# A two-layer attention and FFN kernel on one core: tile work of one sequence placed between the attention steps of the other, records made per key group

## The chip, the cores and the metric

One core of a Trainium2 chip. The time is device microseconds (us) of one execution, the median of the runs shown; less is better. Engines: PE is TensorE, DVE is VectorE, ACT is ScalarE, POOL is GpSimd, SP is SyncE, which issues the transfers. Each runs its own instructions in order, and they wait for each other through semaphores.

## The reference

Input x is 2 sequences of 1024 tokens with 512 features, fp32. Four residual blocks follow each other; attention has 32 query heads of 16 and 8 key/value heads (4 query heads to a key/value head), is causal, and rotates q and k by position. The FFN has one matrix of ±1 and a scale.

```
x = x + attn_a(layernorm(x), w_qkv_a, w_o_a)
x = x + scale * (layernorm(x) @ (2 * kernel - 1))
x = x + attn_b(layernorm(x), w_qkv_b, w_o_b)
x = x + scale * (layernorm(x) @ (2 * kernel - 1))
```

## The kernel before

**Four rounds.** A round is one sequence through one layer; the order is sequence 0 layers a and b, then sequence 1 layers a and b. The whole sequence lives in `xs` (8 tiles of 128 tokens). A round has three stages.

**Stage A** (`SLOTS_A`, one slot per tile): layer norm statistics (`ln_stats` L976, `ln_newton` L990), the transpose of the normed tile, its split into a high part (`hi` L834, ACT) and a low part (`lo` L1009, DVE), the projection to 768 q, k, v columns in three products (`qkv` L572, `multiply` L558), the rotation (`rope_sin` L1204 on POOL, `rope_cos` L1035 and `rope` L1046 on DVE). Then `part_h` L872 (ACT) and `part_l` L1217 (POOL) write a **record** of 64 numbers for each head: the value in parts whose products give fp32 precision. PE transposes a tile's records of all heads in six quads (`turn_rec` L594), and ACT and DVE copy them to `qT` and `kT`, which hold all 8 key groups. Units of group 0 (below) are already made in this stage.

**Groups** 0 to 7, one for each key/value head with its 4 query heads. A **unit** (`unit` L617 on PE, L1052 on DVE) computes scores of a query tile, and DVE reduces them to row maxima (L1068); 22 units make a group. The maxima are split on POOL, transposed on PE (`nm_turn`), copied, and brought by a transfer (`put_nm` L477) as extra rows into `qT`. The **score steps** S.0 to S.17 (`scores` L662) compute scores transposed with the maximum already subtracted; ACT applies Exp to two heads or pairs at a time (L905); POOL cuts diagonal blocks (`mask` L1259); PE multiplies with the values (`pv` L680, ten steps). The output is transposed back (`o_turn`), and divided on DVE (`o_divide`). While group g is in its score steps, the units of g+1 run. The order is written by hand: `GROUP_ORDER` L175, `FIRST_ORDER` L185 for group 0, `LAST_ORDER` L195 for group 7, where no units are left and the first tiles of the next stage stand in their place.

**Tail** (`TAIL_ORDER` L205): per tile the output projection (C: transpose CT, 12 matmuls CP, add), layer norm, FFN (D: transpose DT, 8 matmuls DP, add), with the start of the next round's stage A.

**PSUM.** Of eight banks `psM` has four: in groups they are two pairs, and units, N and O jobs take them by turns (`ring_jobs` L268); a job's pair is free when DVE has read it. In stage A the early units have one of the pairs only (`unit_pair` L256), and the projections the other. `psE` has three banks for score steps, `psO` one for the outputs.

Weights are loaded each round: qkv in one transfer into the `probs` buffer (L467) and split in the tail, the output matrix in four pieces in groups 1 to 4.

Of the kernel before, what the change touches and what calls it, by code (L numbers as in the profile page):

```python
# [37 lines left out]

# [8 lines left out]
RECS = 2  # L47
QUADS = 6
QUAD_ACT = [1, 2, 4, 5]
QUAD_DVE = [0, 3]  # L50

AHEAD = TILES // 2
# [4 lines left out]

CD_TILES = words("C.0 C.1 C.2 C.3 D.0 D.1 C.4 C.5 C.6 C.7 D.2 D.3 D.4 D.5 D.6 D.7")
TURNS = TILES + len(CD_TILES)


def c_turn(t):
    return TILES + CD_TILES.index(("C", t))


def d_turn(t):
    return TILES + CD_TILES.index(("D", t))


assert all(X % 2 == t % 2 for X, (what, t) in enumerate(CD_TILES)) and CD_TILES[-1] == ("D", TILES - 1)


class Signal:

    def __init__(self, sem, credit=0):
        self.sem, self.credit = sem, credit

    def after(self, n):

        return n + (self.credit + 1)  # L90
# [49 lines left out]

# [50 lines left out]
LAST_ORDER = """  # L195
S.0 PV.8.-1 S.1 PV.9.-1 N.1.0 S.2 OC.1.-1 S.3 S.4 PV.0.0
S.5 PV.1.0 S.6 O.1.-1 OC.0.0 PV.2.0 S.7 O.0.0
S.8 CT.0 S.9 PV.3.0 CT.1 S.10 CP.0 PV.4.0
S.11 CT.2 S.12 CP.1 LS.0 S.13 PV.5.0 CT.3 LN.0
S.14 CP.2 S.15 PV.6.0 DT.0 LR.0 S.16 CP.3 S.17 PV.7.0 DT.1 LS.1 LM.0 PV.8.0 PV.9.0  # L200
"""

TAIL_ORDER = """  # L205
DP.0 LN.1 LR.1 O.1.0 DP.1 LM.1 CT.4 CT.5 CP.4 CT.6 CP.5 CT.7 LS.2 T.2 CP.6 T.3 H.2 LN.2 LR.2 LM.2
# [7 lines left out]

# [1135 lines left out]
```

## Time and profile before

| | |
|---|---|
| median of 3 runs | 1418.94 us (1417.74 to 1422.94) |
| profiled execution, span from first to last instruction | 1417.0 us |
| PE busy, weight loads (PEld) | 1296.8 us (92%), 773.8 us (55%) |
| DVE busy | 1039.4 us (73%) |
| ACT busy | 941.6 us (66%) |
| POOL busy | 382.3 us (27%) |
| mean granted clock of PE | 0.988 |

A row of a window view gives, for a stretch of the span, the busy time of each engine in it. A row of the timeline gives a start, a duration from the start of the first to the end of the last instruction of the row, and the instructions merged into it. Matmuls are pipelined and their ends are modelled, so what a matmul costs the engine that is never idle is the distance from its start to the start of the next, not its duration.

### The profile page before, as it was taken

To read this page: it belongs to the slowest core of one execution; us is meant where nothing else is said; L and a number is where in the kernel's file an instruction comes from. 1 tells how busy PE (TensorE), PEld (TensorE's weight loads), DVE (VectorE), ACT (ScalarE), POOL (GpSimd) and SP (SyncE) were. 2 spreads that over 40 slices of the span, in tenths; PEclk is the share of its full clock that TensorE was granted. 3 is DMA by queue.
4 is the path that set the end of the run, shared out by engine and by line. 5 is a ranking of instruction groups with operands and counts; after the bars stand their busy time and mean duration, and the time that the engine had idled before them with its cause. 6 is when DMAs were issued, how large, how long until landed. Compare 5 with 4: busy or idle time off the path is not lost.

```text
span 1417.0 us, 28602 instructions
## 1 busy us (share of the span) xinstructions
PE 1296.8 (92%) x11076; PEld 773.8 (55%) x11076; DVE 1039.4 (73%) x1526; ACT 941.6 (66%) x1770; POOL 382.3 (27%) x591
## 2 busy tenths in 40 slices
PE   5988999989898899998989789999998889999898
PEld 4764444446785444444677444444477744444456
DVE  5667888845767788883566879889266588888737
ACT  4655777774665687776556567877646566877764
POOL 3431222210443122221144222222123422222212
PEclk9999999999999999999999999999999999999999
DMA  3000000001000000000220000000010000000002
GB/s 124 1 1 10 9 18 3 3 2 45 1 1 2 9 13 15 3 2 2 75 90 1 2 10 17 11 2 3 2 45 1 1 2 17 10 10 3 3 6 100
DMA packets 12981, 24.00 MB, mean 17 GB/s; under 512 B 1072, under 2 KB 4144, under 8 KB 12848
## 3 DMA queue, kind: packets, MB, share of 16 engines
q1 hardware_dynamic: 12848, 22.19, 4.7%
q8 instruction: 88, 1.44, 0.4%
q14 instruction: 45, 0.37, 0.1%
HBM read 16.94 MB, written 4.19 MB: 15 GB/s over the span
## 4 chain that ended last, share of the span: by engine, by line
PE 59%; DVE 25%; ACT 7%; issue 5%; POOL 2%; DMA 1%; DVEq 0%; ACTq 0%; SPq 0%; POOLq 0%
DVE mx L1068 18%; PE psO L696 15%; PE psM L560 12%; PE psE L675 12%; PE psM L633 10%; PE psM L543 3%; ACT probs L905 3%; PE psE L613 3%; PE psO L613 2%; PE psM L640 2%; DVE stats L983 2%; POOL attn L1213 1%; DVE qT L1033 1%; DVE xs L1144 1%; ACT xn L823 1%
## 5 line engine op out<-in xcount | busy, mean ns | idle before, releaser
L1068 DVE TENSOR_REDUCE mx<-psM 128x2 f32<-128x768 f32 (+4 forms) x704 | 698.2, 1026 | 113.9 <-PE psM L640 68.4
L905 ACT ACTIVATE probs<-psE 128x512 f32<-128x512 f32 x1152 | 625.5, 595 | 228.5 <-PE psE L675 219.0
L633 PE MATMUL psM<-kT,qT 62*128 62x384 f32 (+5 forms) x1536 | 294.8, 404 | 31.3 <-DVE mx L1068 9.5
L696 PE MATMUL psO<-probs,v_grp 128*32 128x512 f32 (+3 forms) x3072 | 318.5, 503 | 2.3 <-POOL probs L1266 2.2
L1266 POOL TENSOR_SCALAR_AFFINE_SELECT probs<-probs 128x512 f32<-128x512 f32 x256 | 159.3, 634 | 561.7 <-ACT probs L905 527.4
L675 PE MATMUL psE<-qT,kT 64*128 64x512 f32 (+3 forms) x1536 | 279.7, 401 | 32.5 <-ACT probs L905 26.7
L633 PEld LDWEIGHTS psM<-kT,qT 62*128 62x128 f32 x1536 | 146.4, 187 | 179.3 <-DVE mx L1068 133.9
L675 PEld LDWEIGHTS psE<-qT,kT 64*128 64x128 f32 x1536 | 131.3, 186 | 171.2 <-ACT probs L905 126.2
L640 PE MATMUL psM<-mask_b 64*128 64x64 bf16 x2048 | 120.7, 197 | 0.0
L560 PE MATMUL psM<-wq_hi,xT_hi 128*128 128x512 f32 (+1 forms) x384 | 99.1, 380 | 14.7 <-ACT vs L869 9.5
L696 PEld LDWEIGHTS psO<-probs,v_grp 128*32 128x32 f32 x3072 | 68.1, 109 | 65.3 <-issue 36.9
L560 PE MATMUL psM<-w_lo,xT_hi 128*128 128x512 f32 (+1 forms) x384 | 93.6, 366 | 2.0 <-DVE w_lo L1022 2.0
L560 PE MATMUL psM<-wq_hi,xT_lo 128*128 128x512 f32 (+1 forms) x384 | 93.1, 365 | 0.0
L640 PEld LDWEIGHTS psM<-mask_b 64*128 64x128 bf16 x2048 | 60.4, 97 | 56.9 <-issue 25.2
L1213 POOL TENSOR_TENSOR attn<-attn,sin_s 128x320 f32<-128x320 f32 x64 | 66.6, 1061 | 50.8 <-ACT attn L868 50.8
L560 PEld LDWEIGHTS psM<-wq_hi,xT_hi 128*128 128x128 f32 x384 | 62.3, 192 | 28.5 <-issue 18.9
L839 ACT ACTIVATE xT_hi<-psM 128x512 fp32r<-128x512 f32 x64 | 37.8, 597 | 58.5 <-PE psM L543 38.8
L1222 POOL TENSOR_TENSOR probs<-attn,probs 128x512 fp32r<-128x512 f32 x32 | 41.2, 1289 | 125.5 <-ACT probs L880 125.5
L1013 DVE TENSOR_TENSOR xT_lo<-psM,xT_hi 128x512 fp32r<-128x512 f32 x64 | 43.6, 686 | 39.7 <-ACT xT_hi L839 39.1
L613 PE MATMUL psE<-ident,probs 128*128 128x128 f32 x384 | 60.4, 281 | 12.9 <-DVE qT L1033 11.1
L560 PEld LDWEIGHTS psM<-w_lo,xT_hi 128*128 128x128 f32 x384 | 64.8, 191 | 12.9 <-DVE w_lo L1022 2.7
L560 PEld LDWEIGHTS psM<-wq_hi,xT_lo 128*128 128x128 f32 x384 | 65.0, 192 | 9.9
(81 smaller groups left out, 1240.6 us busy)
## 6 DMA issues: line engine op xcount, KB each, us to landing
probs<-in_w_qkv SPq DMA_DIRECT2D x5, 1536.0 KB, 6.4
xs<-in_x SPq DMA_DIRECT2D x8, 512.0 KB, 3.9
xn<-in_w_o SPq DMA_DIRECT2D x16, 256.0 KB, 2.6
out_x<-xs SPq DMA_DIRECT2D x8, 512.0 KB, 2.8
qT<-nm_rows SPq DMA_DIRECT2D x128, 8.0 KB
probs<-in_w_ffn SPq DMA_DIRECT2D x1, 256.0 KB, 7.3
attn<-in_mask SPq DMA_DIRECT2D x1, 160.0 KB, 9.4
sin_s<-in_sin SPq DMA_DIRECT2D x1, 128.0 KB, 6.8
```

What stands on the lines that cost most here:

```text
L543: ins = pe.transpose(dst[:, c * P:(c + 1) * P], src[:, c * P:(c + 1) * P], ident[:])
L560: ins = pe.matmul(dst, xT[:, k, c, :], w[:, c, n0:n1], start=first and i == 0, stop=last and i == len(some) - 1)
L613: ins = pe.transpose(bank[:, n * P:(n + 1) * P], src, ident[:])
L633: return pe.matmul(psM[:, 2 * pair + h % 2, to:to + k1 - k0], qT[lo:lo + MAXROW, g, qt // QT_PER_CHUNK, h // 2, qt % QT_PER_CHUNK * P:(qt ...
L640: return pe.matmul(psM[:, 2 * pair + h % 2, k0:k0 + P // 2], late_b[lo:lo + ROW, half, :], half_b[lo:lo + ROW, :], start=False, stop=half ...
L675: ins = pe.matmul(psE[:, (2 * p + a) % SRING, to:to + w], kT[lo:lo + DEPTH, g, kb * P:(kb + 1) * P], qT[lo:lo + DEPTH, g, c, j // 2, off:o ...
L696: ins = pe.matmul(psO[VW * j:VW * (j + 1), off:off + w], v_grp[:, kb, :], probs[:, (g * NS + s) % PSLOTS, at(j), to:to + w], start=s in (0 ...
L905: act.activation(probs[:, (g * NS + s) % PSLOTS, at(heads[0]):at(heads[0]) + len(heads), 0:w], psE[:, n % SRING, 0:w * len(heads)].rearran ...
L1013: dve.tensor_tensor(xT_lo[:, k].rearrange("p a b -> p (a b)"), src, xT_hi[:, k].rearrange("p a b -> p (a b)").bitcast(F32), ALU.subtract). ...
L1068: dve.tensor_reduce(to, src, AX.X, ALU.max, negate=True).then_inc(ring_used.sem, 1)
L1213: ins = pool.tensor_tensor(t4[:, :, a, :], x4[:, :, 1 - a, :], sn[:, :, a * HALF:(a + 1) * HALF].to_broadcast([P, HEADS + KV, HALF]), ALU. ...
L1266: ins = pool.affine_select(out=d, in_=d, compare_op=ALU.is_ge, fill=0.0, base=0, pattern=[[0, REP], [1, P]], channel_multiplier=-1)
```

## The change

**Rounds.** The order of rounds is now layer a of sequence 0, layer a of sequence 1, layer b of sequence 0, layer b of sequence 1. While round k is in its groups, the other sequence goes, two tiles (a **pair**) at a time, through output projection, FFN and norm of its last attention (where it has one) and the qkv projection of its next (where it has one). So round 0 carries qkv work alone, rounds 1 and 2 all of it, round 3 output and FFN alone. Before the first group stands a prologue (sequence 0's qkv, then records and units of group 0), and behind the last the output work of sequence 1.

**One program for all engines.** A list of words (`PROGRAM`) is made from tables, and each engine walks it and issues its part. `PAIR_ORDER` puts a pair's words behind score steps, counted from the pair's first; pairs begin 26 steps apart, and a round has 144 steps. CT, DT and AT are the transposes of a pair (8 of 128x128), each followed at once by H, its high and low copy (1024 wide); CP has 6 pieces of four matmuls, DP 4, Q 4 for each tile; CA and DA add to x, QC copies q, k, v out; LS, LN, LM are the norm; RO is the rotation.

**PSUM.** `ring_pairs` deals the two pairs of `psM` to all jobs: units, N, O, R, transposes and projections. A projection holds its pair from its first piece to CA, DA or QC, and until then every other job has the other pair alone. In the table of rounds 1 and 2 a pair is held at 56 of 144 steps, and 65 of 176 units, 10 N, 6 O and 7 R jobs fall there; in round 0 it is 24 steps with 27 units, 4 N, 2 O and 5 R; in round 3 (its first seven groups) 32 steps with 38 units, 6 N, 4 O and 2 R.

**Records** are made per group two groups ahead: `PL` (high parts on ACT L853, low on POOL L1110) over all tiles, and three jobs R of 8 transposes each, two copied by ACT and one by DVE, 1024 wide. `qT` and `kT` hold three groups instead of eight. The rotation works in place in `cells`, so its cosine part now waits for POOL's sine part.

**Transfers.** `xs` holds three pairs; x goes through DRAM (`x_mid`) between layers: 24 loads and 16 stores of 512 KB in place of 8 and 8. Weights have buffers of their own and are loaded once for each layer in pieces, 12 after the start in place of 20 transfers.

The core of the diff (the tables and what deals out PSUM):

```diff
-GROUP_ORDER = """
-U.0 U.1 S.0 N.1.0 PV.8.-1 S.1 U.2 PV.9.-1 OC.1.-1 S.2 U.3 U.4 S.3 U.5 S.4 PV.0.0 S.5 U.6 U.7 PV.1.0
-S.6 U.8 O.1.-1 S.7 U.9 PV.2.0 OC.0.0 U.10 S.8 U.11 PV.3.0 U.12 S.9 O.0.0 S.10 U.13 N.0.1 S.11 U.14
-U.15 S.12 PV.4.0 U.16 S.13 U.17 PV.5.0 U.18 S.14 U.19 PV.6.0 S.15 U.20 U.21 S.16 PV.7.0 S.17 X
-"""
+GROUP_ORDER = """
+U.0 S.0 N.1.0 PV.8.-1 U.1 S.1 U.2 PV.9.-1 V OC.1.-1 S.2 U.3 S.3 U.4 U.5 S.4 PV.0.0 S.5 U.6 PV.1.0 U.7
+S.6 U.8 O.1.-1 S.7 U.9 PV.2.0 OC.0.0 U.10 S.8 K.0 U.11 PV.3.0 U.12 S.9 O.0.0 S.10 U.13 N.0.1 PL S.11 U.14
+U.15 S.12 PV.4.0 U.16 S.13 U.17 PV.5.0 U.18 S.14 R.0 U.19 PV.6.0 S.15 R.1 U.20 U.21 S.16 R.2 PV.7.0 S.17 X K.1
+"""
+START, PERIOD = 7, 26
+PAIR_ORDER = """
+0 LX CT H.CT | 2 CP.0 | 3 CP.1 | 4 CP.2 | 5 CP.3 | 6 CP.4 | 7 CP.5 CA LS.D | 9 LN.D LM.D | 10 DT H.DT | 12 DP.0 | 13 DP.1 | 14 DP.2
+| 15 DP.3 DA ST LS.A | 17 LN.A LM.A | 18 AT H.AT | 19 Q.0.0 | 20 Q.0.1 | 21 Q.0.2 | 22 Q.0.3 QC.0 | 23 Q.1.0 RO.0 | 24 Q.1.1 | 25 Q.1.2
+| 26 Q.1.3 QC.1 | 28 RO.1
+"""
...
+def ring_pairs():
+
+    pair_of, before, held, newest, turn = {}, {}, {}, [None, None], 1
+    for w in PROGRAM:
+        what = w[0]
+        job = None
+        if what in ("U", "N", "O", "R", "CT", "DT", "AT"):
+            job = w
+        elif what in ("CP", "DP") and w[2] == 0:
+            job = w[:2]
+        elif what == "Q" and w[3] == 0:
+            job = w[:3]
+        if job is not None:
+            turn = 1 - turn if 1 - turn not in held.values() else turn
+            assert turn not in held.values(), w
+            pair_of[job], before[job], newest[turn] = turn, newest[turn], job
+            if what not in ("U", "N", "O", "R"):
+                held[job] = turn
...
-        xs = sb("xs", [P, TILES, DIM])
+        xs = sb("xs", [P, XSLOTS, 2, DIM])
...
-        qT = sb("qT", [P, KV, CHUNKS, REP // 2, QCHUNK], F32R)
-        kT = sb("kT", [P, KV, SEQ], F32R)
+        qT = sb("qT", [P, 3, CHUNKS, REP // 2, QCHUNK], F32R)
+        kT = sb("kT", [P, 3, SEQ], F32R)
...
+            def part_h(G):
+                r, g = G // KV, G % KV
+                src = by_group(cells, r, g)
+                act.wait_ge(rope_ready, ROPE_NO[r * PAIRS + PAIRS - 1, 1] + 1)
```

**PE in a group in mid round.** L675 and L749 are score steps, L633 and L708 with L640 and L715 the units and their masks, L696 and L769 the value products, L660 the transposed maxima. Before:

```order
L675 MATMUL psE<-qT,kT 128x384 x2
L675 MATMUL psE<-qT,kT 128x128 x2
L696 MATMUL psO<-probs,v_grp 32x512 x4
L633 MATMUL psM<-kT,qT 128x448 x2
L675 MATMUL psE<-qT,kT 128x512 x2
L633 MATMUL psM<-kT,qT 128x448 x2
L640 MATMUL psM<-mask_b 128x64 x4
```

Now, in round 1 (L622 is a piece of a projection, L780 the transposed output):

```order
L749 MATMUL psE<-qT,kT 128x512 x2
L622 MATMUL psM<-wq_hi,xT_hi 128x512 x4
L708 MATMUL psM<-kT,qT 128x320 x2
L780 MATMUL psM<-ident,o_T 128x128 x4
L749 MATMUL psE<-qT,kT 128x512 x2
L622 MATMUL psM<-wq_lo,xT_hi 128x512 x4
L708 MATMUL psM<-kT,qT 128x320 x2
L715 MATMUL psM<-mask_b 128x64 x4
L769 MATMUL psO<-probs,v_grp 32x256 x4
L708 MATMUL psM<-kT,qT 128x384 x2
L749 MATMUL psE<-qT,kT 128x512 x2
L622 MATMUL psM<-wq_hi,xT_lo 128x512 x4
```

A piece of four matmuls stands behind each score step, and its bank pair is not given back before the last piece has been copied out.

**DVE in the same part of a group.** L1068 and L1026 are the reductions of units. Before:

```order
L1068 TENSOR_REDUCE mx<-psM 128x2
L1081 CAST nm_rows<-psM 32x128
L1068 TENSOR_REDUCE mx<-psM 128x2 x8
L1074 TENSOR_TENSOR mx<-mx 128x16
L1068 TENSOR_REDUCE mx<-psM 128x2x2 x2
```

Now, in round 1 (L1001 and L1003 are the rotation, L974 a low copy, L1008 the copy of the key records):

```order
L1026 TENSOR_REDUCE mx<-psM 128x2 x2
L1001 TENSOR_TENSOR cells<-cells,cos_s 128x8x80
L1003 TENSOR_TENSOR cells<-cells,t_s 128x8x80
L1026 TENSOR_REDUCE mx<-psM 128x2 x4
L974 TENSOR_TENSOR xT_lo<-psM,xT_hi 128x1024
L1026 TENSOR_REDUCE mx<-psM 128x2 x2
L1008 CAST kT<-psM 128x1024
L1001 TENSOR_TENSOR cells<-cells,cos_s 128x8x80
L1003 TENSOR_TENSOR cells<-cells,t_s 128x8x80
L1032 TENSOR_TENSOR mx<-mx 128x16
```

The reductions, which stood in one row of eight, now have rotation, low copy and record copy between them.

## Rows read from the trace of the kernel before

**Rows 1.** The page: span, and busy time of each engine.
```profile
span 1417.0 us, 28602 instructions
PE 1296.8 (92%) x11076; PEld 773.8 (55%) x11076; DVE 1039.4 (73%) x1526; ACT 941.6 (66%) x1770; POOL 382.3 (27%) x591
```

**Rows 2.** Windows: prologue; groups 0 and 4; group 7 to next group 0; the end.
```profile
core 0: us, PE busy (x) PEld busy (x) DVE busy (x) ACT busy (x) POOL busy (x), PEclk, DMA share, GB/s
0.00:101.60 101.60, 78.99 (x521) 65.05 (x523) 61.12 (x103) 54.36 (x101) 38.86 (x44) 0.97 0.13 44
101.60:135.60 34.00, 27.75 (x285) 14.06 (x283) 28.74 (x34) 20.14 (x37) 6.21 (x14) 0.96 0.04 10
...
217.40:244.00 26.60, 25.83 (x267) 12.60 (x267) 23.58 (x30) 20.93 (x39) 7.35 (x14) 1.00 0.02 4
...
297.20:449.70 152.50, 138.29 (x916) 102.89 (x909) 88.65 (x171) 88.97 (x171) 46.81 (x50) 1.00 0.03 12
1341.10:1417.00 75.90, 67.30 (x399) 44.07 (x391) 37.52 (x90) 41.56 (x80) 12.54 (x13) 1.00 0.14 50
```

**Rows 3.** Timeline of PE in group 4: start, us, engine, line, operation.
```profile
218.17 0.49 PE L675 MATMUL psE<-qT,kT 64*128 64x512 f32 x2
218.50 0.35 PE L633 MATMUL psM<-kT,qT 62*128 62x384 f32 x2
...
218.86 1.06 PE L696 MATMUL psO<-probs,v_grp 128*32 128x512 f32 x8
219.86 0.50 PE L675 MATMUL psE<-qT,kT 64*128 64x384 f32 x4
220.20 0.39 PE L633 MATMUL psM<-kT,qT 62*128 62x384 f32 x2
...
220.50 0.47 PE L633 MATMUL psM<-kT,qT 62*128 62x512 f32 x2
```

**Rows 4.** Waits in group 4: who for whom, us, times, longest.
```profile
PEld psM L633 <- DVE mx L1068: 4.3, 9, 0.8
```

**Rows 5.** Timeline of DVE in group 4.
```profile
218.97 0.96 DVE L1068 TENSOR_REDUCE mx<-psM 128x2 f32<-128x768 f32 x1 [0.30 <-PE psM L640]
```

**Rows 6.** Chain of waits in the first 102 us: pieces of projections.
```profile
51.68 0.93 PE psM L560 x4
...
55.28 1.43 PE psM L560 x12
```

**Rows 7.** Timeline of PE in stage A: transposes of records.
```profile
54.24 0.60 PE L613 MATMUL psE<-ident,probs 128*128 128x128 f32 x4
54.68 0.60 PE L613 MATMUL psO<-ident,probs 128*128 128x128 f32 x4
```

**Rows 8.** Groups by line and shape: mean ns behind the busy us.
```profile
L1068 DVE TENSOR_REDUCE mx<-psM 128x2 f32<-128x1024 f32 x192 | 225.4, 1217 | 4.6 <-PE psM L633 4.2
...
L1213 POOL TENSOR_TENSOR attn<-attn,sin_s 128x320 f32<-128x320 f32 x64 | 66.6, 1061 | 50.8 <-ACT attn L868 50.8
...
L1013 DVE TENSOR_TENSOR xT_lo<-psM,xT_hi 128x512 fp32r<-128x512 f32 x64 | 43.6, 686 | 39.7 <-ACT xT_hi L839 39.1
...
L1042 DVE TENSOR_TENSOR attn<-attn,cos_s 128x640 f32<-128x640 f32 x32 | 27.7, 867 | 57.8 <-ACT attn L868 56.9 <-DVE var_eps L988 0.9
...
L1144 DVE SCALAR_TENSOR_TENSOR xs<-psM,rstd,xs 128x512 f32<-128x512 f32 x32 | 23.9, 747 | 3.0 <-DVE var_eps L988 2.3 <-DVE rstd L1000 0.7
```

**Rows 9.** Timeline of DVE: a norm's statistics, and the last steps of its Newton iteration.
```profile
340.68 0.15 DVE L994 TENSOR_TENSOR newton<-rs 128x2 f32<-128x2 f32 x1
...
341.60 0.22 DVE L1000 SCALAR_TENSOR_TENSOR rstd<-rs,scale_s,newton 128x2 f32<-128x2 f32 x1
...
349.51 1.27 DVE L983 BATCH_NORM_STATS2 stats<-xs 128x6 f32<-128x512 f32 x2
...
351.33 0.17 DVE L988 TENSOR_SCALAR var_eps<-mv 128x2 f32<-128x2 f32 x1
```

**Rows 10.** DMA issues: count, size and us to landing.
```profile
xs<-in_x SPq DMA_DIRECT2D x8, 512.0 KB, 3.9
```

More of the change, by code:

```diff
@@ L46 @@
 DEPTH = ROW
[L47 to L55, printed above, removed]
+ROUNDS = BATCH * LAYERS
+GROUPS = ROUNDS * KV
+SSTEPS = 18
+FIRST_PAIR, LAST_PAIR = -1, ROUNDS
+XSLOTS = 3
+CELL = (REP + 2) * HD
+QKCELL = (REP + 1) * HD
+GW = REP * HD
+RJOBS_ACT = 2
 def words(text):
     return [(w.split(".")[0], *(int(a) for a in w.split(".")[1:])) for w in text.split()]
[L64 to L90, printed above, removed]
 def score_steps():
@@ new lines, in pair_word @@
+def pair_word(q, name):
+    what, *arg = name.split(".")
+    arg = [int(a) if a.isdigit() else a for a in arg]
+    if what == "H":
+        return [(what, (arg[0], q))]
+    if what in ("LS", "LN", "LM"):
+        return [(what, (arg[0], q))]
+    if what in ("CT", "DT", "AT"):
+        return [(what, q)]
+    if what == "CP" and not arg:
+        return [(what, q, i) for i in range(6)]
+    if what == "DP" and not arg:
+        return [(what, q, i) for i in range(4)]
+    if what == "Q" and len(arg) == 1:
+        return [(what, q, arg[0], i) for i in range(4)]
+    return [(what, q, *arg)]
@@ new lines, in prepare_words, with program @@
+def prepare_words(text):
+    out = []
+    for what, *arg in words(text):
+        out.append((what, *arg) if what in ("PL", "V", "R") else (what, 0, *arg))
+    return out
+def program():
+    out = edge_words(PROLOGUE, FIRST_PAIR) + prepare_words(PREPARE)
+    middle = middle_words()
+    for G in range(GROUPS - 1):
+        out += group_words(G, GROUP_ORDER, middle)
+    assert not middle, sorted(middle)
+    return out + edge_words(LAST_ORDER, LAST_PAIR) + edge_words(TAIL_ORDER, LAST_PAIR)
@@ L552, in products @@
-            def products(k, his, los, n0, n1):
-                return [(xT_hi, w, c, n0, n1) for w in (his, los) if w is not None for c in range(KC)] + [
-                    (xT_lo, his, c, n0, n1) for c in range(KC)]
-            def multiply(k, dst, some, first, last):
-                for i, (xT, w, c, n0, n1) in enumerate(some):
-                    ins = pe.matmul(dst, xT[:, k, c, :], w[:, c, n0:n1], start=first and i == 0,
-                                    stop=last and i == len(some) - 1)
-                return ins
@@ L955, in _, with norm @@
-            ln_apply(0, 0)
-            first_rstd(0, 0)
-            hi(0, 0, psE[:, 0, :])
-            for c in range(KC):
-                wq_split(0, c)
-            rounds(act, round_)
+            def norm(e, q):
+                what, i = e, NORM_NO[e, q]
+                job = earlier_turn((what + "T", q), ("DT", "AT"))
+                if job is not None:
+                    act.wait_ge(turned, TURN_NO[job] + 1)
+                act.wait_ge(var_ready, i + 1)
+                for n in range(2):
+                    ins = act.activation(xn[buffer_of(q)][:, n, :], xs[:, q % XSLOTS, n, :], ACT.Identity, bias=mv[:, i % 2, n, 0:1], scale=-1.0)
+                ins.then_inc(xn_ready, 1)
```

1483 lines of the change are left out of this document (701 added, 782 removed).

## The prediction

> **What bounds the kernel now.** First the engines' sums: PE is busy 92% of the span, DVE 73%, ACT 66% [rows 1]. Then the windows, to see that the stages have different limits [rows 2]. A group in the middle takes 26.60 us with PE busy 25.83 and DVE 23.58. The stretch from the start of group 7 to the start of the next round's group 0 takes 152.5 us with PE busy 138.3, but DVE only 88.7 and ACT 89.0. The matter is what PE needs, since its busy time is modelled, so I went to the timeline. A score step costs 0.33 us from start to next start (218.17 to 218.50), or 0.34 with two parts; a unit with its mask 0.30 (220.20 to 220.50), a longer one up to 0.4; a value product of 512 columns 1.00 [rows 3]. For a group: 18 score steps x 0.34 = 6.1; 22 units x 0.37 = 8.1; ten value products, eight at 1.0 and two of half the columns at 0.57 (estimate) = 9.1; two N and two O jobs about 1.0. Sum 24.3 us, 91% of 26.60. So in a group PE (24.3) and DVE (23.6) are both near full, and PE stands still for short waits on DVE: 4.3 us of weight loads waiting for a reduction, mostly under running matmuls [rows 4].
>
> In the stretch between: four matmuls of 512 columns cost 0.93 us, twelve of 256 columns 1.43 [rows 6], four transposes 0.44 [rows 7]. The qkv projection of a tile is 3 x 0.93 + 1.43 = 4.22, of eight 33.8; output projection 24 x 0.93 = 22.3; FFN 16 x 0.93 = 14.9; 24 transposes of tiles x 0.44 = 10.6; 48 of records x 0.44 = 21.1; group 7 without units 16.2; the units of group 0 8.1. Sum 127 us of 152.5, that is 83%. The rest is PE waiting in chains of copies. This is what the change can win, together with the slow group 0 (34.00 us) [rows 2], four times each.
>
> The Trainium skill (Perfetto Trace Analysis, Identifying the Most-Contended Engine) says that matmul busy time doesn't tell how near TensorE is to its limit, and that the busy share of weight loads does. The trace agrees with the first half: 25.83 us busy against 24.3 needed. By the second, with weight loads at 55%, the time would go by DVE; that is a rival below.
>
> **The change, part by part.** Work is neither added nor removed on PE except for batching: transposes go in eights, 2 x 0.44 = 0.88.
>
> *PE.* Groups: 8 x 24.3 = 194.4 per round. Records, 24 jobs x 0.88 = 21.1. Round 0 also carries qkv, 33.8, and four pair transposes, 3.5: 252.8. Rounds 1 and 2 carry everything, 71.0, and twelve pair transposes, 10.6: 297.1 each. Round 3 has seven groups here, 170.1, 18 record jobs 15.8, output and FFN 37.2, eight pair transposes 7.0: 230.1. Together 1077.1 us between the first score step and the last group.
>
> *DVE.* A group stays at 23.58 [rows 2]. The copy of key records, 1024 wide, I price as a reduction of 1024 from PSUM, 1.22 [rows 8]. A norm takes 2.0 for statistics (349.51 to 351.50) and 1.14 for Newton (340.68 to 341.82) [rows 9]; a low copy of 1024, 1.22; adding the output projection 1.22; the FFN's 2 x 0.75; the rotation, two passes like the 0.87 one, 1.73 for each tile [rows 8]. A pair thus adds 3.1 + 1.2 + 3.5 = 7.8 in round 0, 6.3 + 3.7 + 1.2 + 1.5 + 3.5 = 16.2 in rounds 1 and 2, 3.1 + 2.4 + 1.2 + 1.5 = 8.2 in round 3. Rounds: 8 x 24.8 + 31 = 229; 263; 263; 7 x 24.8 + 33 = 207. DVE is below PE in each. Where it was 97% of PE's need in a group, it is 89% in rounds 1 and 2. Two new waits sit in its queue with all reductions behind them: for ACT's high copy at each pair's turn (48 times; now 39.1 us for 64 and shorter ones [rows 8]), and for POOL's sine, two of 1.06 us [rows 8], once a tile.
>
> *ACT and POOL* have room: ACT 20.93 of 26.60, POOL 7.35 [rows 2]. ACT gains per group about 4 us of record parts and record copies, and 4 us of copies and norms, for a group that gets 10 us longer. POOL gets the sine, 2.1 us a tile, ahead of masks; the value product of a step comes two or three score steps after its mask is asked for, over 4 us, which covers it. Without this cover PE would wait up to 2 us a tile, 24 times.
>
> *SP.* 24 more transfers of x, each landing in about 4 us [rows 10]; a load is asked for six score steps before it is used, over 8 us, so I cost it at nothing. The stores stand before later transfers of maxima, but their data are ready when SP comes to them.
>
> *The bank pairs.* Held steps: 56 + 56 + 24 + 32 = 168 of 558. A unit then waits for the reduction of the unit before. From its start to DVE's start is 0.47 us (218.50 to 218.97) [rows 3, 5], the reduction about 1.03 (23.6 with little else, for 22), 0.1 back: 1.6. In round 1: 65 x 1.6 + 10 N x 0.75 + 6 O x 1.4 + 7 R x 2.1 = 135 us of chain, against PE's need at these 56 steps, 56 x 1.35 + 6.2 + 70.8 = 153. PE has enough else to do (a score step and a piece are 1.3 us, the reduction 1.0), so the chain is mostly covered, but not where two units stand together or only a value product is between them. This eats what DVE's lighter load gives.
>
> So how full will PE be? Ends: 83% as in the stretch between (chains everywhere), and 94% (the shortest waits only). I take 90%, just under the group's 91%, since that row has the same in-order mix: 1077.1 / 0.90 = 1197.
>
> *The ends.* Prologue: 18 us to the first full projection, as now; eight tiles at 4.22 + 0.44 and small stalls, 40; rotation, parts and records of group 0 in a chain, 13; its 22 units alone, bound by DVE, 23.6 / 0.9 and a record copy, 28: 99, against 101.6. Last group and output work are as before, by pairs instead of tiles: 78 against 75.9. Together 177. The wins there are nothing.
>
> Sum: 1197 + 177 = 1374 us of span, against the profiled 1417.0. The median is 1.9 above that span, so **1376**.
>
> **The rivals.**
>
> 1. *PE fuller.* The pieces fill every wait of attention, and PE stands at 94%: 1146 + 177 = 1323. For it: DVE's share falls from 97% to 89% of PE's. Against: the two new waits and held pairs. 0.17.
> 2. *DVE is the limit, not PE* (the skill's rule above, read from the weight loads). DVE's rounds are 962 us; at the 89% of a group, 1081 + 177 = 1258. Against: a value product of 512 columns costs 1.00 us whatever waits. 0.08.
> 3. *The gain goes into chains.* In-order coupling stays at 87%, between group and stretch: 1238 + 177 = 1415, no change that can be told (about 0.5%, 7 us, is what a measurement of this kernel can tell). 0.10.
> 4. *Slower: one pair of banks binds.* Where a pair is held, pieces don't run under reductions but ahead of them. The forecast has 153 / 0.9 = 170 us for 56 held steps, 3.0 a step. With DVE's rotations and adds in the chain, 135 + 23, and half of the 71 us of pieces outside it, it is 194, or 3.46 a step. That is 0.43 x 168 = 72 more: 1446. It turns slower than before from 3.3 a step. Before, every job in a group could rotate through two pairs; nothing in the trace shows a group's units on one. 0.15.
>
> The Trainium skill (Perfetto Trace Analysis, Matmuls) asks that independent groups of matmuls rotate through different PSUM banks, so that the evacuation of one runs under the matmuls of the next. That speaks for rival 4, which breaks this at 30% of the steps.
>
> **How the numbers follow.** The forecast, PE between 88% and 92%, has 0.50. Faster: 0.50 + 0.17 + 0.08 = 0.75; no change 0.10; slower 0.15. The low end leaves out rival 2 and the best of rival 1, the high end the worse half of rival 4: 1308 to 1436. The forecast's own range is 1348 to 1401.
>
> **What would show it.** Right: the round from first score step to first score step is about 281 us for round 0, 330 for 1 and 2; PE's waits in them are short and on DVE; the time to the first score step is near 99. Held steps near 3.0 us, others near 1.8. Wrong: rounds 1 and 2 over 345 with weight loads of units waiting for reductions (rival 4), or below 315 (rivals 1 and 2, the second with DVE at 89% busy); PE waiting for masks or for maxima brought by transfers, which I cost at nothing.

## The result, and the profile after

| | before | after |
|---|---|---|
| median of 4 runs | 1420.72 us | 1850.41 us (1848.78 to 1857.28) |
| ratio, 95% interval | | 1.304 (1.3015 to 1.3066) |
| profiled span | 1417.0 us | 1849.7 us |
| mean granted clock of PE | 0.988 | 0.903 |

The change makes the kernel 30% slower; 1376 was forecast. From the page of the changed kernel, the counterpart of [rows 1]: the sums, and the row of PE's granted clock in 40 slices, in tenths.

```profile
span 1849.7 us, 28067 instructions
...
PE 1474.2 (80%) x11072; PEld 817.5 (44%) x11072; DVE 1041.2 (56%) x1415; ACT 905.8 (49%) x1601; POOL 334.3 (18%) x565
...
PEclk9769898998998989888999898988889988999999
```

No engine got more work: PE has 11072 matmuls where it had 11076, DVE is busy for 1041 us where it was 1039. Yet PE's busy time is 177 us longer, and PE's idle time is 375 us where it was 120, 255 more. These two make up the 433 us between the spans. Most of the 177 us is the clock: in the trace 311.5 us of PE's busy time lie in stretches at the lower level, before 32.5, and half of the difference, about 140 us (an estimate), is by how much those matmuls would be shorter at full clock.

The windows after: time to the first score step; the four rounds, each from its first score step to the next one's (the fourth without its last group); then three single groups, and the end. Columns as in [rows 2].

```profile
0.00:113.40 113.40, 75.78 (x399) 59.00 (x399) 58.01 (x90) 29.54 (x44) 23.86 (x33) 0.78 0.11 39
113.40:485.30 371.90, 303.06 (x2525) 162.16 (x2525) 228.28 (x295) 212.19 (x378) 88.41 (x144) 0.92 0.05 14
485.30:955.00 469.70, 375.05 (x2769) 203.20 (x2768) 258.84 (x353) 224.64 (x398) 79.65 (x137) 0.89 0.04 11
955.00:1425.80 470.80, 372.12 (x2769) 202.70 (x2768) 259.64 (x352) 225.52 (x400) 82.96 (x140) 0.90 0.04 12
1425.80:1755.30 329.50, 277.00 (x2222) 145.30 (x2226) 204.22 (x265) 178.27 (x320) 54.44 (x103) 0.93 0.04 15
731.90:807.50 75.60, 58.08 (x379) 32.69 (x380) 35.16 (x48) 29.57 (x51) 11.38 (x19) 0.84 0.05 15
919.40:955.00 35.60, 31.99 (x291) 15.79 (x290) 25.07 (x30) 23.71 (x44) 8.01 (x15) 0.90 0.01 2
1727.60:1755.30 27.70, 25.33 (x258) 11.94 (x262) 23.01 (x29) 20.41 (x38) 6.05 (x13) 1.00 0.01 3
1755.30:1849.70 94.40, 71.20 (x395) 45.09 (x389) 32.23 (x63) 35.64 (x63) 4.98 (x8) 0.96 0.13 45
```

The loss is in the rounds: 372, 470, 471 and 330 us, where 281, 330, 330 and 256 (230.1 / 0.90) were forecast. The three groups show it in steps. The group from 1727.6 has neither tile work nor records and takes 27.7 us, near the 26.60 of before [rows 2]. The one from 919.4 makes records but has no tile work: 35.6 at a clock of 0.90, though PE has only three jobs of 0.88 us more. The one from 731.9 has both: 75.6.

What the engines wait for in the whole span (us, times, longest), to set beside [rows 4]; the weight load before a unit is where PE meets a reduction that is late:

```profile
DVE mx L1026 <- PE psM L715: 248.3, 233, 4.1
PEld psM L708 <- DVE mx L1026: 223.7, 237, 4.4
...
PE psM L708 <- DVE mx L1026: 106.1, 83, 4.1
...
DVE xT_lo L974 <- ACT xT_hi L839: 85.3, 35, 8.8
...
DVE cells L1001 <- POOL t_s L1107: 53.0, 23, 5.0
...
DVE newton L962 <- ACT rs L831: 47.1, 32, 2.2
...
PE psM L708 <- DVE xT_lo L974: 30.9, 29, 1.5
...
PE psM L708 <- ACT qT L868: 25.0, 29, 1.1
```

PE and DVE wait for each other, by turns. The last two rows are units that wait until a pair is freed by the low copy of a tile's transpose, or by ACT's copy of records. Before, the same weight loads waited 133.9 us, at most 1.0 at a time. One such place on DVE, in the group from 731.9:

```profile
738.87 1.41 DVE L989 SCALAR_TENSOR_TENSOR xs<-psM,rstd,xs 128x512 f32<-128x512 f32 x2 [1.70 <-PE psM L622]
740.65 1.29 DVE L951 BATCH_NORM_STATS2 stats<-xs 128x6 f32<-128x512 f32 x2 [0.37 <-DVE xs L989]
...
742.48 0.65 DVE L956 TENSOR_SCALAR var_eps<-mv 128x2 f32<-128x2 f32 x1
743.27 3.22 DVE L1026 TENSOR_REDUCE mx<-psM 128x2 f32<-128x768 f32 x3
748.65 0.16 DVE L962 TENSOR_TENSOR newton<-rs 128x2 f32<-128x2 f32 x1 [2.16 <-ACT rs L831]
```

and on PE beside it:

```profile
740.69 0.48 PE L749 MATMUL psE<-qT,kT 64*128 64x384 f32 x4
741.01 0.45 PE L708 MATMUL psM<-kT,qT 62*128 62x512 f32 x2
...
744.28 0.79 PE L708 MATMUL psM<-kT,qT 62*128 62x512 f32 x2 [2.74 <-DVE mx L1026]
...
745.73 1.93 PE L769 MATMUL psO<-probs,v_grp 128*32 128x512 f32 x8
```

From 738.87 on DVE adds the FFN's output and takes the statistics. Units already stand in both pairs, but their reductions come only at 743.27, behind that work. PE, never more than two pairs ahead, stands for 2.74 us. Then eight matmuls of a value product last 1.93 us, which is 1.06 at full clock [rows 3]: the clock is at its lower level, 1.2 GHz. At 748.65 DVE has itself waited 2.16 us for ACT's inverse roots.

### The profile page after: what moved, and what is told of

Read it like the earlier page. It is cut to its first block, busy times and chain, and to the rows that moved or that the text cites. A ratio compares the mean times of both kernels' runs of the same rounds, so it can differ in the third digit from the quotient of the medians.

```text
span 1849.7 us, 28067 instructions
## 1 busy us (share of the span) xinstructions
PE 1474.2 (80%) x11072; PEld 817.5 (44%) x11072; DVE 1041.2 (56%) x1415; ACT 905.8 (49%) x1601; POOL 334.3 (18%) x565
## 4 chain that ended last, share of the span: by engine, by line
PE 60%; DVE 19%; ACT 12%; issue 6%; POOL 2%; DVEq 0%; DMA 0%; ACTq 0%; POOLq 0%
PE psM L622 17%; PE psO L769 13%; PE psM L708 11%; DVE mx L1026 10%; PE psE L749 9%; ACT probs L877 4%; PE psM L692 4%; PE psM L607 2%; POOL t_s L1107 2%; DVE xT_lo L974 2%; ACT xT_hi L839 2%; PE psM L715 2%; ACT qT L868 2%; DVE stats L951 1%; ACT xn L823 1%
## 5 line engine op out<-in xcount | busy, mean ns | idle before, releaser
L1026 DVE TENSOR_REDUCE mx<-psM 128x2 f32<-128x768 f32 (+4 forms) x704 | 708.4, 1027 | 424.7 <-PE psM L715 248.3
L708 PE MATMUL psM<-kT,qT 62*128 62x384 f32 (+5 forms) x1536 | 338.2, 452 | 208.4 <-DVE mx L1026 106.1
L769 PE MATMUL psO<-probs,v_grp 128*32 128x512 f32 (+3 forms) x3072 | 356.0, 554 | 1.0 <-POOL probs L1148 0.6
L708 PEld LDWEIGHTS psM<-kT,qT 62*128 62x128 f32 x1536 | 156.0, 200 | 445.8 <-DVE mx L1026 223.7
L749 PE MATMUL psE<-qT,kT 64*128 64x512 f32 (+3 forms) x1536 | 291.7, 418 | 32.3 <-ACT probs L877 31.1
L749 PEld LDWEIGHTS psE<-qT,kT 64*128 64x128 f32 x1536 | 142.0, 202 | 160.3 <-issue 91.8
L692 PE MATMUL psM<-ident,recs 128*128 128x128 f32 x768 | 116.0, 301 | 25.7 <-DVE mx L1026 11.5
L715 PE MATMUL psM<-mask_b 64*128 64x64 bf16 x2048 | 126.9, 204 | 0.0
L692 PEld LDWEIGHTS psM<-ident,recs 128*128 128x128 f32 x768 | 94.6, 154 | 50.0 <-issue 19.5
L769 PEld LDWEIGHTS psO<-probs,v_grp 128*32 128x32 f32 x3072 | 70.3, 114 | 76.5 <-issue 57.7
L974 DVE TENSOR_TENSOR xT_lo<-psM,xT_hi 128x1024 fp32r<-128x1024 f32 x42 | 51.4, 1223 | 85.5 <-ACT xT_hi L839 85.3
L715 PEld LDWEIGHTS psM<-mask_b 64*128 64x128 bf16 x2048 | 64.7, 102 | 65.1 <-issue 41.0
L868 ACT ACTIVATE qT<-psM 128x1024 fp32r<-128x1024 f32 x64 | 65.6, 1024 | 43.1 <-PE psM L692 42.9
L607 PE MATMUL psM<-ident,xn 128*128 128x128 f32 x256 | 45.9, 338 | 27.6 <-ACT xn L823 15.9
L1107 POOL TENSOR_TENSOR t_s<-cells,sin_s 128x320 f32<-128x320 f32 x64 | 53.8, 861 | 77.8 <-ACT cells L850 77.8
L622 PE MATMUL psM<-wq_hi,xT_hi 128*128 128x512 f32 (+1 forms) x224 | 57.0, 379 | 9.2 <-ACT wq_hi L903 4.1
L780 PE MATMUL psM<-ident,o_T 128*128 128x128 f32 x256 | 43.7, 297 | 21.3 <-DVE mx L1026 15.3
L823 ACT ACTIVATE xn<-xs,mv 128x512 f32<-128x512 f32 x64 | 42.6, 719 | 35.4 <-DVE mv L954 35.4
```

What stands on the lines that cost most here:

```text
L622: ins = pe.matmul(dst, left[:, c, :], w[:, c, n0:n1], start=first and c == 0, stop=last and c == KC - 1)
L692: ins = pe.transpose(banks(job)[:, a, n * P:(n + 1) * P], src, ident[:])
L708: return pe.matmul(to_banks[:, h % 2, to:to + k1 - k0], qT[lo:lo + MAXROW, G % 3, qt // QT_PER_CHUNK, h // 2, qt % QT_PER_CHUNK * P:(qt % ...
L715: return pe.matmul(to_banks[:, h % 2, k0:k0 + P // 2], late_b[lo:lo + ROW, half, :], half_b[lo:lo + ROW, :], start=False, stop=half == 1)
L749: ins = pe.matmul(psE[:, (2 * p + a) % SRING, to:to + w], kT[lo:lo + DEPTH, G % 3, kb * P:(kb + 1) * P], qT[lo:lo + DEPTH, G % 3, c, j // ...
L769: ins = pe.matmul(psO[VW * j:VW * (j + 1), off:off + w], v_grp[:, G % 2, kb, :], probs[:, (G * NS + s) % PSLOTS, at(j), to:to + w], start= ...
```

## The experiments

Thirteen kernels, in five batches, each batch with its own runs of the kernel before (1416.71 to 1419.37 us). The two theories of the first batch: A, a pair held over many steps makes PE and DVE take turns; B, what stands ahead of the reductions on DVE, and of the exps on ACT, does it whether a pair is held or not. Each later expectation says what its own letters (C to H) stand for.

**1. No hold over steps.** All pieces of a job behind one score step, so that a projection has its pair for one step.

```diff
-0 LX CT H.CT | 2 CP.0 | 3 CP.1 | 4 CP.2 | 5 CP.3 | 6 CP.4 | 7 CP.5 CA LS.D | 9 LN.D LM.D | 10 DT H.DT | 12 DP.0 | 13 DP.1 | 14 DP.2
-| 15 DP.3 DA ST LS.A | 17 LN.A LM.A | 18 AT H.AT | 19 Q.0.0 | 20 Q.0.1 | 21 Q.0.2 | 22 Q.0.3 QC.0 | 23 Q.1.0 RO.0 | 24 Q.1.1 | 25 Q.1.2
-| 26 Q.1.3 QC.1 | 28 RO.1
+0 LX CT H.CT | 3 CP CA LS.D | 5 LN.D LM.D | 8 DT H.DT | 12 DP DA ST LS.A | 14 LN.A LM.A | 17 AT H.AT | 21 Q.0 QC.0 | 23 RO.0 | 26 Q.1 QC.1 | 28 RO.1
```

> Edit to the changed kernel: all pieces of a projection job stand behind one score step, so its bank pair is never held over a score step; the amount of work is the same. Theory A (the held pair: units alone on one pair wait for DVE, and for whatever DVE does ahead of the reduction): the waits go, and with them the half clock, 1850 falls to 1400 to 1520. Theory B (the mix itself costs, wherever the pieces stand, since every engine works in order): it stays over 1700.

Measured 1824.59 us, 1.2872 (1.2835 to 1.2909); rounds 368, 467, 456, 324; clock 0.879. Only 26 us better, in theory B's range. A alone does not carry the loss.

**2. Filler.** The score matmuls of each step with a held projection three times.

```diff
-                    scores(*arg)
+                    scores(*arg, times=FILL if tuple(arg) in HELD_STEPS else 1)
```

> Edit to the changed kernel: in the score steps at which a projection holds a pair, the score matmuls are issued three times over (same values into the same bank), about 0.46 to 0.7 us more for PE at each of some 160 steps. If half of the loss is the clock that falls while PE stands still (theory C), PE is kept busy where it waited anyway, and the time falls to 1700 to 1780 with a granted clock above 0.95. If PE itself is short of time at these steps, the fillers are paid: 1920 to 1950. If the waits are long enough to hide the fillers and the clock is no matter, 1850 within 20.

Measured 1958.75 us, 1.3818 (1.3681 to 1.3956); clock 0.900. The filler cost 108 us, somewhat more than its range for a PE that is short of time: it did not fit into PE's waits, and did not bring the clock back.

**3. Thin pieces.** One matmul in place of four; three quarters of the projections' products are left out.

```diff
-                for c in range(KC):
+                for c in range(1):
```

> Edit to the changed kernel: each piece of a projection issues one matmul in place of four, which leaves three quarters of all projection products out (about 213 us of PE work at full clock, 160 of them behind score steps). Theory A: in held steps PE waits for the pair anyway, so less than half of it comes back: 1740 to 1850. Theory B or a PE that is the limit: all of it and more comes back, 1550 to 1640.

Measured 1804.79 us, 1.2732 (1.2676 to 1.2789). 1056 matmuls fewer save 46 of the expectation's 213 us, in theory A's range. But the mean clock falls to 0.810 with them, so the run does not part the work of PE from its clock.

**4. Small tile work on DVE.** Waits and order stay.

```diff
-                    ins = dve.bn_stats(stats[:, i % 2, n, :], xs[:, slot, n, :])
+                    ins = dve.bn_stats(stats[:, i % 2, n, :], xs[:, slot, n, 0:64])
...
-                dve.tensor_tensor(to, flat(("CP", q)), to, ALU.add).then_inc(wo_added, 1)
+                dve.tensor_tensor(to[:, 0:64], flat(("CP", q))[:, 0:64], to[:, 0:64], ALU.add).then_inc(wo_added, 1)
```

> The changed kernel with the tile work on DVE (and POOL's half of the rotation) cut to slices: low copies over 64 of 1024 columns (after the first eight), both adds, the statistics over 64 of 512 columns, and the rotation over one of the cells' eight groups. What is left out: most of the split, the residual, the statistics and the rotation; the output is not the reference's. PE's instructions, all waits and the order stay. Theory D (DVE works in order, so the tile work's long instructions stand ahead of the row maxima, and PE, which may be only two pairs of banks ahead, runs dry): PE's idle before row-maximum units, 107 us after the change, falls under 40, and with the clock that comes back the time falls to 1600 to 1700 us. Rival F (the long hold of bank pairs by PE's own pieces and ACT's copies is what binds; DVE's size does not matter): 1800 to 1840.

Measured 1691.80 us, 1.1937 (1.1902 to 1.1972); clock 0.942. 159 us less, 136 of them between the first score step and the last group, in theory D's range. That is what the length of the tile work cost, which the prediction put at nothing: DVE's for the most part, though the edit also cuts POOL's part of the rotation, for which DVE waited (53.0 us). The sign that theory D gave came out weaker: PE's waits before units fell from 106.1 us to 60.9, not under 40.

```profile
PE psM L708 <- DVE mx L1027: 60.9, 70, 2.3
```

**5. Small records.** Groups 4 to 31; the cut shown is that of the transposes, the copies and the parts on ACT and POOL are cut likewise.

```diff
-                for a in range(2):
-                    for n in range(QT_PER_CHUNK):
+                for a in range(2 if G < 4 else 1):
+                    for n in range(QT_PER_CHUNK if G < 4 else 1):
```

> The changed kernel with the records of key groups 4 to 31 made small: one transpose in place of eight in each of the three jobs, copies of 128 in place of 1024 columns, the parts of one tile in place of eight on ACT and POOL. What is left out: seven eighths of each record; the output is not the reference's. Waits and order stay. Theory D (records per group cost what their instructions last, on ACT's queue above all): the groups that have records and no tile work fall from 35 us to 28 to 30, and the time by 5 to 7 us for each of 28 groups, to 1660 to 1710 us. Rival F (it is the places of the three jobs in the turn of the two pairs that cost, whatever their size): 34 us in such a group, 1810 to 1840.

Measured 1815.91 us, 1.2813 (1.2776 to 1.285); clock 0.881. The groups with records alone fell from between 34.8 and 36.4 to between 30.3 and 31.4 us, near theory D's 28 to 30, but the whole by 35 us only, which is in rival F's range. Groups with tile work gained less or nothing (the group of 75.6 us fell to 70.3, its like in the next round to 74.6); why is not shown.

**6. Waits taken from DVE's head, copies parted.** DVE's rotation two steps behind POOL's, low copies one step behind the high ones, statistics behind the adds.

> The changed kernel's work whole, with only places moved: DVE's part of the rotation two steps behind POOL's, the low copies one step behind ACT's high copies, the statistics one step behind the adds, the Newton step later. So DVE has no instruction at the head of its queue that waits for POOL or ACT, and never two long ones together. Theory D: the waits for POOL (53 us) and for ACT's high copy (85 us) go from DVE's list, and the time falls by 60 to 130 us, to 1720 to 1790. Rival F (the time that DVE works, not what it waits for, is in the way): under 30 us less, 1820 to 1850.

Measured 1843.52 us, 1.3008 (1.297 to 1.3045): 7 us. The low copy is what frees a pair after a transpose, so this edit also held pairs longer, and the run does not tell the two apart. Experiment 12 does.

**7. Both small** (the edits of 4 and 5).

> The slices of the kernel with small tile work on DVE and the small records of groups 4 to 31 together (output not the reference's, as in those two). Theory D: both gains add, since they lie in different places: 1400 to 1530 us, the share of the span at the low clock level under 8%. Rival F: 1750 or more.

Measured 1623.51 us, 1.1455 (1.1406 to 1.1504); clock 0.943. With DVE's work small, the records are worth 68 us more. But this is 93 us above theory D's range: 207 us over the kernel before remain with DVE busy only 54% of the span. So there is a third cost.

**8. Trials in the kernel before.** Whatever the change mixes, its parts can be put one at a time into single groups of the kernel before, where a group is 26.60 us.

```diff
-                out.append((job, turn % 2))
+                out.append((job, 0 if g == 2 else turn % 2))
...
                             unit(g + 1, arg[0])
+                            if (g, arg[0]) in ((4, 5), (4, 15), (6, 9)):
+                                for again in range(2 if g == 6 else 1):
+                                    k = (g - 4) + again if g == 6 else arg[0] // 15
+                                    dve.tensor_reduce(extra[:, r, k:k + 1], xs[:, 0:2, :].rearrange("p a n -> p (a n)"), AX.X, ALU.max)
```

> The kernel before, its output unchanged, with three small trials in single key groups of each round. In group 2 every unit, transpose and rescaling uses the first pair of banks only. In group 4 two extra reductions over 1024 columns (some 1.2 us each, into a scratch) stand on DVE behind units 5 and 15; in group 6 two of them stand directly behind each other, behind unit 9. A plain group is 26.6 us. Theory G (with one pair free, PE and DVE take turns): group 2 lasts 36 to 45 us, so 0.5 to 1.0 us more for each of its 18 steps. If pairs do not matter it stays under 29. Theory D (a DVE instruction in the row stalls PE for its own length): groups 4 and 6 last 28.5 to 29.2 us. If DVE's 3.6 us of slack in a group hide it: 26.6 to 27.2. The whole kernel: 1417 + 4 x (14 + 2.4 + 2.4) = 1490 by G and D, 1420 by neither.

Measured 1538.41 us, 1.0841 (1.0787 to 1.0894). Windows: a plain group; two extra reductions apart; the same two together; all jobs of a group on one pair (round 1).

```profile
269.00:295.60 26.60, 25.83 (x267) 12.55 (x267) 23.59 (x30) 20.43 (x39) 6.09 (x13) 1.00 0.01 3
240.90:269.00 28.10, 26.12 (x267) 12.61 (x267) 25.59 (x32) 20.93 (x39) 7.37 (x14) 1.00 0.01 3
295.60:326.40 30.80, 27.92 (x246) 12.89 (x250) 24.76 (x30) 20.45 (x39) 6.09 (x13) 0.89 0.01 2
544.40:589.80 45.40, 32.59 (x267) 14.56 (x267) 24.57 (x30) 21.11 (x39) 7.32 (x14) 0.81 0.02 7
```

Two reductions of 1.21 us cost 1.5 us when they stand apart. Together (2.33 us) they cost 4.2 in every round: behind them PE stands still for 1.59 us, and then the clock is at its lower level, 1.2 GHz, from 311.0 to 317.8. The unit that waited, and windows of the stretch before it and of the slow one:

```profile
309.81 0.45 PE L634 MATMUL psM<-kT,qT 62*128 62x384 f32 x2 [1.59 <-DVE mx L1069]
307.00:311.00 4.00, 2.14 (x20) 0.81 (x19) 4.00 (x5) 1.49 (x4) 1.03 (x3) 1.00 0.00 0
311.00:317.80 6.80, 6.80 (x39) 3.23 (x39) 4.40 (x7) 3.94 (x8) 0.83 (x2) 0.50 0.01 2
```

And one pair for a whole group costs 18.8 us in two rounds (22 in the others), with no work added: 1.04 us a step at least, just above theory G's range. Here its mechanism is shown by itself, with its clock: of the 18.8 us PE's idle time is 12.0 (12.81 against 0.77) and its longer busy time, at 0.81, is 6.8.

**9. Everything small** (3 with 7), and **10. small without holds** (1 with 7).

> The changed kernel with everything small at once: one matmul in place of four in each piece, DVE's tile work on slices, the records of groups 4 to 31 small (output not the reference's). Waits, order and holds of the pairs stay. Theory G (holding one pair makes PE and DVE take turns, whatever PE does in the pieces): with the small DVE work and records and whole pieces the full rounds took 403 and 407 us; they stay at 370 to 400, the time at 1500 to 1600. Theory H (PE's pieces cost what they last, since PE can put nothing behind them): rounds of 330 to 350 us, the time 1380 to 1430.

> The order with all pieces of a job behind one score step, so that no pair stays held over steps except from a transpose to its copies, with DVE's small tile work and the small records (output not the reference's). Theory G: the holds are gone, so rounds fall from 403 us to 350 to 370, the time to 1450 to 1500. Theory H: PE's work in the pieces is the same, rounds 390 to 410, 1590 to 1640 us.

Measured 1617.99 us, 1.1401 (1.1288 to 1.1515) for 9, and 1603.78 us, 1.1301 (1.1246 to 1.1356) for 10. In 9 three quarters of the work of the pieces is gone and the time stays, as theory G says; its number was still too low. Between the first score step and the last group the time even rises, from 1438.6 us in 7 to 1476.0, while the ends get shorter. But the clock falls to 0.798, and the run does not tell the turns from the clock. In 10 the holds are gone and the time stays too, in theory H's range: in blocks, the pieces cost what they last (the steps with a whole block and no transpose took 6.6 us on average in rounds 1 and 2, PE busy for 6.3 of it).

**11. Pieces in the kernel before.** Real pieces of four matmuls ahead of score steps, with and without a held pair.

```diff
+def held(g, step):
+
+    return g == 5 or (g in (4, 6) and 6 <= step < 12)
+
+
+def has_piece(g, step):
+
+    return g in (3, 5) or (g in (2, 4) and 6 <= step < 12)
...
-                out.append((job, turn % 2))
+                out.append((job, 0 if held(g, step) else turn % 2))
...
+                    if has_piece(g, p):
+                        for kc in range(KC):
+                            pe.matmul(psE[:, 2 * p % SRING, :], xT_hi[:, 0, kc, :], wf_s[:, kc, :], start=kc == 0, stop=kc == KC - 1)
```

> The kernel before, its output unchanged, with trials in single groups. A piece is four matmuls of 512 columns in front of a score step, 1.06 us, as in a projection; its result is overwritten by the scores. Group 2: pieces in six steps (6 to 11). Group 3: pieces in all 18. Group 4: pieces in six steps while one pair is held. Group 5: both in all 18. Group 6: one pair held in six steps, no pieces. A plain group is 26.6 us with 2.3 us of it free on PE. If pieces alone simply add (PE is full anyway): group 2 gets 4 to 6.4 us longer, group 3 17 to 19 us, to 44 to 46. Theory G (hold dearer than its piece): group 6 gets 6 to 7.5 us longer though it has no work more. Both together: if the piece fits into the wait of the hold, group 4 is 33 to 35 and group 5 46 to 49, no more than with the hold alone; if they add, group 4 is 38 to 40 and group 5 60 to 65 us. The first would say that the changed kernel's excess is in holds and clock, the second that it is a plain sum of piece and hold.

Measured 1733.41 us, 1.2214 (1.2142 to 1.2286). Windows of groups 2 to 6: six pieces; 18 pieces; six of both; 18 of both; six holds.

```profile
160.10:194.90 34.80, 34.02 (x295) 17.25 (x295) 24.63 (x30) 21.06 (x40) 7.32 (x14) 1.00 0.04 10
194.90:240.90 46.00, 44.84 (x335) 23.81 (x334) 23.22 (x29) 21.11 (x39) 7.33 (x14) 1.00 0.02 7
240.90:280.10 39.20, 34.20 (x295) 17.29 (x295) 25.03 (x30) 21.04 (x39) 7.37 (x14) 1.00 0.01 3
280.10:333.40 53.30, 45.47 (x335) 24.00 (x334) 23.80 (x29) 20.65 (x39) 6.09 (x13) 1.00 0.01 1
333.40:369.90 36.50, 29.47 (x246) 12.97 (x250) 23.09 (x28) 20.64 (x39) 6.09 (x13) 0.86 0.01 2
```

| over a plain group of 26.6 us | 6 steps | 18 steps |
|---|---|---|
| piece | 8.2 us, 1.37 a step | 19.4 us, 1.08 a step |
| held pair | 9.9 us, 1.65 a step | 18.8 to 22 us (8), 1.04 to 1.22 a step |
| both | 12.6 us, 2.1 a step | 26.7 us, 1.48 a step |

A piece alone costs its whole length, at a clock of 1.00: there was no gap for it. A hold alone costs about as much as a piece, part of it through the clock (0.86 with six holds). Together they cost less than their sum but more than either: with six steps the group, 39.2 us, is in the range of the rival that adds them, with 18 steps, 53.3, between the two. One difference from the change remains: here a piece stands ahead of the score step and in its bank of `psE`, there behind it and in the held pair. PE's timeline in group 5 (both) shows what is left of the turn:

```profile
296.14 1.20 PE L686 MATMUL psE<-wf_s,xT_hi 128*128 128x512 f32 x4
297.26 0.50 PE L691 MATMUL psE<-qT,kT 64*128 64x512 f32 x2
297.60 0.31 PE L646 MATMUL psM<-kT,qT 62*128 62x320 f32 x2
298.92 0.63 PE L556 MATMUL psM<-ident,o_T 128*128 128x128 f32 x4 [1.01 <-DVE mx L1084]
299.30 1.18 PE L686 MATMUL psE<-wf_s,xT_hi 128*128 128x512 f32 x4
```

The piece stands in front of the step (L686), the unit (L646) and the next job (L556) behind it. The piece covers the reduction before the unit, and nothing covers the one before L556, so PE waits 1.01 us there.

**12. Waits taken from DVE's head, copies kept together**, and **13. the same, with both small.**

```diff
-0 LX CT H.CT | 2 CP.0 | 3 CP.1 | 4 CP.2 | 5 CP.3 | 6 CP.4 | 7 CP.5 CA LS.D | 9 LN.D LM.D | 10 DT H.DT | 12 DP.0 | 13 DP.1 | 14 DP.2
+0 LX CT H.CT | 2 CP.0 | 3 CP.1 | 4 CP.2 | 5 CP.3 | 6 CP.4 | 7 CP.5 CA | 8 LS.D | 9 LN.D | 10 DT H.DT | 12 LM.D DP.0 | 13 DP.1 | 14 DP.2
-| 15 DP.3 DA ST LS.A | 17 LN.A LM.A | 18 AT H.AT | 19 Q.0.0 | 20 Q.0.1 | 21 Q.0.2 | 22 Q.0.3 QC.0 | 23 Q.1.0 RO.0 | 24 Q.1.1 | 25 Q.1.2
-| 26 Q.1.3 QC.1 | 28 RO.1
+| 15 DP.3 DA ST | 16 LS.A | 17 LN.A | 18 AT H.AT | 19 Q.0.0 | 20 LM.A Q.0.1 | 21 Q.0.2 | 22 Q.0.3 QC.0 | 23 Q.1.0 RO.0 | 24 Q.1.1 | 25 Q.1.2 RD.0
+| 26 Q.1.3 QC.1 | 28 RO.1 | 30 RD.1
```

(RD is DVE's part of the rotation, RO POOL's.)

> The changed kernel's work whole; only words moved so that DVE does not stand before something that ACT or POOL still has to make, with row maxima behind it: the Newton step three steps after the inverse roots it reads (before: in the same step), DVE's part of the rotation two steps after POOL's, the statistics one step after each addition. High and low copies stay together, so no pair is held longer than in the change. If those waits of DVE carry the loss: 50 to 120 us less, 1730 to 1800. If the length of DVE's work, the turns and the held pieces carry it: 1820 to 1850.

> The same moved words with the small tile work on DVE and the small records (output not the reference's). With the words in their old places this was 1623 us, and its trace shows DVE idle for 2.2 us before a Newton step and PE idle for 3.1 us after it. If waits at the head of DVE's queue are what is left there: 1540 to 1590. If it is holds, turns and the pieces' own length: 1600 to 1625.

Measured 1783.12 us, 1.2556 (1.242 to 1.2692), and 1598.28 us, 1.1254 (1.1133 to 1.1376). With all work kept, 67 us go, in the range for waits at DVE's head. The edit also parts the additions from the statistics, so it takes long DVE instructions asunder too. The waits of DVE of kernel 12:

```profile
DVE xT_lo L979 <- ACT xT_hi L844: 102.2, 40, 6.2
...
DVE cells L1006 <- POOL t_s L1112: 18.0, 5, 5.2
...
DVE newton L967 <- ACT rs L836: 10.0, 8, 1.9
```

The waits for POOL and for the inverse roots fell from 53.0 and 47.1 us to 18.0 and 10.0. In 13 only 25 us go, so with DVE's work small these waits matter less.

No variant of the changed kernel, those with most of the tile work left out included, came within 12% of the kernel before.

## Why the prediction was wrong

**The step that failed** is "1077.1 / 0.90 = 1197". The mid part took 371.9 + 469.7 + 470.8 + 329.5 = 1641.9 us, so PE ran at 66% of its need, not 90%. It was reasoned from a row of a group that has neither a held pair, nor other work among the reductions, nor half clock. Trials 8 and 11 give the share for some of these. Priced as in the prediction (24.3 us for a group, 0.93 for a piece), 18 pieces alone run at 41.0 of 46.0, 89%. Pieces with held pairs run at 41.0 of 53.3, 77%; held pairs without pieces at 24.3 of 45.4, 54%.

The need itself was too small as well. The 0.93 us for a piece came from the prologue [rows 6]; among score steps a piece takes 1.12 from its start to the next start (296.14 to 297.26 in trial 11), and in the change it is the same (the median at full clock). The middle has 192 pieces of four 512-column matmuls, so about 36 us are missing from the 1077 (an estimate). With 1.12, the 18 pieces alone run at 44.5 of 46.0, 97%: their 89% was a low price, not slack.

**Where the time went.** Counted from the starts of the score steps in the trace of the change, the 168 held steps took 3.66 us on average against 3.0, about 105 us over the forecast; the other 390 took 2.63 against 1.8, about 340 over it. So three quarters of the middle's miss of 445 us lie where no pair of banks was held at the score step. The 36 steps with a pair's transpose took 5.4 us; the 312 with neither a piece nor a transpose 2.24.

**"The chain is mostly covered."** I compared the sum of the chain (135 us) with the sum of PE's other work (153 us). But cover must stand at the place of the wait: a piece stands in one place of a step, and where two jobs of the other pair follow it, the second waits. Measured 1.48 to 2.1 us over a plain step of 1.48, so 2.96 to 3.58 a held step against 3.0; held steps in the change took 3.7 in rounds 1 and 2. Rival 4 had this mechanism and a fair price for it alone (72 us more); the trials give 67 to 123 us over the pieces' own cost for 168 steps, and the count above 105. It was a seventh to a quarter of the miss of 474 us.

**"DVE is below PE in each"**, so its tile work was costed at nothing. The sums were right (DVE 228, 259, 260 and 204 us busy, forecast 229, 263, 263 and 207), the use of them wrong. DVE's work was not hidden under PE's, since PE may be only two pairs ahead: whatever stands on DVE between two reductions for longer than that lead stops PE. Experiment 4 prices its length at 159 us (with POOL's part of the rotation), 12 the waits at its head at 67; the two overlap, since with small work the moved words gave only 25 (13). "Two new waits sit in its queue" named two of the right places and gave them no price; the third, Newton behind ACT's norm, I did not name.

**"ACT and POOL have room."** Records cost 7.9 us in a group (35.6 against 27.7) where 2.6 of PE were counted. Their copies sit between exps on ACT while a pair waits for them: units on PE waited 25.0 us for `qT` copies in the span. Made small, they give back 35 us alone and 68 with DVE's work small.

**The clock** had no term. It is 1.00 in groups 2 to 6 of every round before, but not in group 1, here with group 2:

```profile
135.60:164.30 28.70, 27.80 (x267) 12.95 (x267) 23.27 (x30) 20.95 (x40) 7.29 (x14) 0.92 0.04 12
164.30:190.90 26.60, 25.84 (x267) 12.58 (x267) 23.59 (x30) 20.95 (x40) 7.30 (x14) 1.00 0.04 12
```

So the trace of before had its price too, 2.1 us in a group at 0.92. In the change it was 0.89 to 0.93 in the rounds. How much of the time this is cannot be read off: the stretches at the lower level last 359 us in all, before 35, and half of the difference is 162 us, but part of the slower work fills waits, and no run has the waits without the clock.

**The ends** were 113.4 + 94.4 = 207.8 us, not 177: the prologue's mean clock is 0.78 against 0.97 [rows 2]. With small DVE work and records the first part took 100.0, at 0.82.

By removal, 159 us (tile work on DVE) and 68 (records) make 227 of the 430 us. The other 203 (207 against the kernel before of that batch) did not go with thinner pieces, with blocks, or with moved words (25 at most). In rounds 1 and 2 of kernel 7, the 138 steps with pieces and no transpose take 3.14 us on average, which lies in the range of trial 11 (2.96 to 3.58), and the 24 with a pair's transpose 4.96, of which PE was busy 3.6. So the pieces at their full length, with turns, account for part of the 203; in the transposes' steps of the change units waited 30.9 us for the low copy that frees the pair. What the transposes cost by themselves was not tried, and stays open.

The rule of the Trainium skill (Perfetto Trace Analysis, Matmuls) that independent matmul groups should rotate through different PSUM banks agrees with trial 8: one pair cost at least 18.8 us a group. The Trainium skill (Perfetto Trace Analysis, Identifying the Most-Contended Engine) takes the busy share of weight loads, beside the share of peak FLOPs, as the measure of how near TensorE is to its limit. In a group that share was 47% (12.60 of 26.60 us) [rows 2], yet 18 pieces added their whole length (trial 11), so the weight loads alone did not show that PE was nearly full. Rival 2, built on them, came out wrong: DVE was busy 56% of the span, not 89%.
